# Moving the dense projections of three batched attentions to other heads, with V, k and output later in the narrow ones

## The reference

```python
x = x + jnp.tanh(g_xattn[1]) * _L1_xattn_ref(_layernorm(x, axis=-1), ctx_1024, ctx_1024, mask_BxS2_if1, 1, ...)
x = x + jnp.tanh(g_ffn[1]) * _L1_ffn_ref(_layernorm(x, axis=-1), ...)
```

```python
xn = _layernorm(x, ln_gamma, ln_beta)
q = (xn @ w_q).reshape(B, SQ, NUM_HEADS, DIM_HEAD)
kv = context @ w_kv
k, v = jnp.split(kv, 2, axis=-1)
...
scores = jnp.einsum('bqhd,bkhd->bhqk', q * SCALE, k)
attn = jax.nn.softmax(scores, axis=-1)
out = jnp.einsum('bhqk,bkhd->bqhd', attn, v).reshape(B, SQ, INNER)
out = out @ w_out + b_out
return out * jnp.tanh(gate[0])
```

## Time and profile before

| what | us |
|---|---|
| median of three runs | 3197.92 (3197.83 to 3222.6) |
| the profiled execution | 3205.33 |
| its span in the trace | 3203.5 |
| mean granted TensorE clock in it | 0.884 |
| PE busy, share of the span | 2656.1, 83% |
| DVE | 1589.6, 50% |
| ACT | 1262.7, 39% |
| POOL | 1249.5, 39% |

### The profile page before, as it was taken

One profiled execution on the slowest core, in us unless ns is written; L12 is line 12 of the kernel. 1 busy time (PEld: TensorE's weight loads), 2 busy tenths in 40 slices (PEclk: granted clock), 3 DMA queues, 4 the chain that ended last, 5 costly groups with the idle time before them and its releaser, 6 DMA issues. The chain is left out here.

```text
span 3203.5 us, 56229 instructions
## 1 busy us (share of the span) xinstructions
PE 2656.1 (83%) x18095; PEld 2431.6 (76%) x18096; DVE 1589.6 (50%) x3633; ACT 1262.7 (39%) x3098; POOL 1249.5 (39%) x1190
## 2 busy tenths in 40 slices
PE   4674479489989999869997289998899999789997
PEld 4574468388978888769896178887788888678887
DVE  3665545566625444455552234444677767333334
ACT  3232135144443333234444134443666666433332
POOL 0012461565322845032203555541354453284334
PEclk9786689698869999978885599999899999799999
DMA  3031244211001433110001233321000000042322
GB/s 114 1 132 47 81 159 134 61 46 40 9 30 54 145 95 111 40 44 28 28 8 40 86 101 108 118 80 40 17 22 19 13 13 7 27 142 90 111 69 89
DMA packets 128101, 207.99 MB, mean 65 GB/s; under 512 B 16576, under 2 KB 88412, under 8 KB 127728
## 3 DMA queue, kind: packets, MB, share of 16 engines
q1 hardware_dynamic: 63920, 119.94, 12.1%
q10 hardware_dynamic: 50064, 47.18, 4.6%
q0 software_dynamic: 13872, 37.66, 3.7%
HBM read 147.67 MB, written 57.02 MB: 64 GB/s over the span
## 5 line engine op out<-in xcount | busy, mean ns | idle before, releaser
L535 ACT ACTIVATE moe_act<-moe_gu 128x256 f32<-128x256 f32 (+1 forms) x431 | 189.3, 439 | 621.8 <-PE moe_gu L95 621.7
L93 PE MATMUL moe_gu<-moe_whi,moe_xThi 128*128 (+2 forms) x1018 | 409.6, 402 | 14.3 <-POOL moe_wlo L320 14.3
L93 PE MATMUL moe_yp<-moe_whi,moe_hThi 128*128 (+1 forms) x1238 | 394.1, 318 | 5.9 <-DVE moe_hTlo L821 5.6
L95 PE MATMUL moe_gu<-moe_whi,moe_xTlo 128*128 (+2 forms) x1018 | 390.3, 383 | 0.0
L94 PE MATMUL moe_gu<-moe_wlo,moe_xThi 128*128 (+2 forms) x1018 | 389.7, 383 | 0.0
L320 POOL TENSOR_TENSOR moe_wlo<-moe_raw,moe_whi 128x768 fp32r<-128x768 f32 (+1 forms) x174 | 350.5, 2015 | 37.8 <-issue 13.8
L94 PE MATMUL moe_yp<-moe_wlo,moe_hThi 128*128 (+1 forms) x1238 | 349.1, 282 | 0.0
L95 PE MATMUL moe_yp<-moe_whi,moe_hTlo 128*128 (+1 forms) x1238 | 349.0, 282 | 0.0
L821 DVE TENSOR_TENSOR moe_hTlo<-moe_tp,moe_hThi 128x256 fp32r<-128x256 f32 (+1 forms) x431 | 210.4, 488 | 236.5 <-ACT moe_hThi L541 234.8
L805 DVE TENSOR_TENSOR moe_h<-moe_act,moe_gu 128x256 f32<-128x256 f32 x321 | 135.0, 421 | 376.6 <-ACT moe_act L535 372.0
L318 POOL CAST moe_whi<-moe_raw 128x768 fp32r<-128x768 f32 (+1 forms) x174 | 156.5, 899 | 320.8 <-DMA moe_raw<-in_moe_w 320.3
(11 more groups left out here) (472 smaller groups left out, 6931.5 us busy)
## 6 DMA issues: line engine op xcount, KB each, us to landing
moe_raw<-in_moe_w SPq DMA_DIRECT2D x118, 384.0 KB, 3.2
moe_raw<-in_moe_w SPq DMA_DIRECT2D x56, 512.0 KB, 4.6
moe_xr<-rows_x ACTq DMA_DIRECT2D x69, 256.0 KB, 2.7
rows_y<-moe_y ACTq DMA_DIRECT2D x69, 256.0 KB, 2.2
rows_x<-att_zeros SPq DMA_DIRECT2D x16, 512.0 KB, 6.4
att_cT_hi<-ctxT_hi SPq DMA_DIRECT2D x24, 256.0 KB, 2.7
att_cT_lo<-ctxT_lo SPq DMA_DIRECT2D x24, 256.0 KB, 2.9
moe_xr<-rows_x ACTq DMA_DIRECT2D x41, 128.0 KB, 2.0
```

The source lines that it names most:

```text
L93: pe.matmul(out, lhs[0], rhs[0], start=first, stop=False, **kw)
L95: return pe.matmul(out, lhs[1], rhs[0], start=False, stop=last, **kw)
L535: act.activation(act_sb[i % 2][:, :], gu[i % 2][:, 0:HC], func).then_inc(act_done, 1)
```

## The change

In `wide_phase`:
- `kT` 3 and `qT` 3 of a batch are computed in its own heads 0 and 1, not in heads 13 and 14 of the one before. The other rounds move so that no head has more than one, but head 4, which has both `nT`; `V1` goes from heads 2 and 3 to 5 and 6. The context `cT` of the next batch is loaded after `V1`, as before.
- The output projection becomes two rounds at heads 2 and 3, one for each tile, in the banks `r_ps`. DVE adds each tile to x as its step of the round, ACT only reads a column of the bank into `seen`. `x_done` and its wait are gone; `o_hi` of the first pair waits until PE has done the second output round.
- The statistics for MoE are made at head 14 in place of 4; the expert rows are taken after heads 8, 10, 12 and 13 in place of 6, 12, 14 and 15; POOL makes the inverse roots at heads 14 and 15 of the batch before, and normalises at heads 0 and 1 in place of 1 and 2; its `add_bias` goes from head 9 to 10.

In `small_phase`:
- `v` goes from head 1 of its batch to head -3. Without rotation, `k` goes from -9 to -14 and `out` from 35 to 40 (from head 3 to head 8, two batches on). V has three buffers.
- The expert rows of batch 3 and later are taken 5 to 9 heads earlier: (-29, -26, -25, -25) for K = 2 and (-26, -25, -21, -16, -16) for K = 3. Batch 2 has its own list.
- POOL does `aux` for q and k ahead of `norm`.
- The statistics for MoE stand behind the round `out`.

The diff, cut to its core:

```diff
-    ROUNDS = [(4, "nT", 0), (5, "nT", 1), (7, "qT", 0), (8, "kT", 0), (8, "qT", 1), (9, "kT", 1), (10, "V0", 0), (10, "qT", 2),
-              (11, "kT", 2), (12, "V0", 1), (13, "qT", 3), (14, "kT", 3)]
-    OWN = [(2, "V1", 0), (3, "V1", 1)]
-    FIRST = [*(("kT", part) for part in range(4)), ("V0", 0), ("V0", 1), ("nT", 0), ("nT", 1), *(("qT", part) for part in range(4))]
+    ROUNDS = [(4, "nT", 0), (4, "nT", 1), (7, "qT", 0), (8, "kT", 0), (9, "qT", 1), (10, "kT", 1), (11, "V0", 0), (12, "V0", 1),
+              (13, "qT", 2), (14, "kT", 2)]
+    OWN = [(0, "kT", 3), (1, "qT", 3), (2, "out", 0), (3, "out", 1), (5, "V1", 0), (6, "V1", 1)]
+    FIRST = [*(("kT", part) for part in range(3)), ("V0", 0), ("V0", 1), ("nT", 0), ("nT", 1), *(("qT", part) for part in range(3))]
     PRO = len(ROUNDS)
...
-        TAKE = dict(zip((*((6, 12) if K == 2 else (6, 8, 12)), 14, 15), PIECES))
+        TAKE = dict(zip((*range(10 - 2 * (K - 1), 12, 2), 12, 13), PIECES))
...
-                    if h % 4 == 0:
+                    if h == 12:
+                        wait_own(pe, rd_done, i, lo, 0, "qT", 3, last)
+                    elif h % 4 == 0:
...
-                        if g == 1:
-                            wait(pe, x_done, i, lo, 1, s // H)
...
-                def project(i, lo, nxt):
-                    wait(pe, ol_done, i, lo, NGR, (nxt + 1) * NGR)
-                    out = o_ps[1][:, :].rearrange("p (t d) -> p t d", t=TB)
-                    for t in range(TB):
-                        for c in range(OC):
-                            mm = mm3(pe, out[:, t, :], [a[:, c, t * P:(t + 1) * P] for a in OT], [a[:, c, :] for a in wo], c == 0, c == OC - 1)
-                    mm.then_inc(out_ready, 1)
+                def project(bank, t):
+                    for c in range(OC):
+                        mm = mm3(pe, bank, [a[:, c, t * P:(t + 1) * P] for a in OT], [a[:, c, :] for a in wo], c == 0, c == OC - 1)
...
                     wait(pe, rd_done, i, lo, NRD, a + pos - 1)
-                    if kind == "nT":
+                    if kind == "out":
+                        if lo == 0:
+                            mm = pe.transpose(bank[:, 0:P], ident[:, :], ident[:, :])
+                        else:
+                            wait(pe, ol_done, i, lo, NGR, 0)
+                            mm = project(bank[:, 0:D], part)
...
-                        wait(act, out_ready, i, lo, 1, turn)
+                        wait(act, rd_ready, i, lo, NRD, PRO + turn * NRD + [r[1:] for r in BODY].index(("out", 1)) + 1)
...
+                    if kind == "out":
+                        act.activation(seen[:, part:part + 1], bank[:, 0:1], ACT.Copy).then_inc(rd_hi, 1)
...
-                def residual(b):
-                    v.wait_ge(out_ready, b + 1)
-                    v.wait_ge(biased, b + 1)
-                    out = o_ps[1][:, :].rearrange("p (t d) -> p t d", t=TB)
-                    v.scalar_tensor_tensor(x_of(b), out, tg[:, 0:1], x_of(b), ALU.mult, ALU.add).then_inc(x_done, 1)
+                def residual(b, t, src):
+                    if t == 0:
+                        v.wait_ge(biased, b + 1)
+                    xt = x[:, TB * b + t, :]
+                    return v.scalar_tensor_tensor(xt, src, tg[:, 0:1], xt, ALU.mult, ALU.add)
...
+                        if i == 0:
+                            v.drain().then_inc(rd_done, 1)
+                        else:
+                            residual(i - 1, part, bank[:, 0:D]).then_inc(rd_done, 1)
...
-                        if h == 3 and i > 0:
-                            residual(i - 1)
-                        if h == 4 and i > 0:
+                        if h == 14 and i > 0:
                             moments(i - 1)
...
-                        if i < B - 1:
-                            if h == 0:
-                                roots(i + 1, 0)
-                                roots(i + 1, 1)
-                            if h in (1, 2):
-                                norm(i + 1, 2 * h - 2)
-                                norm(i + 1, 2 * h - 1)
-                        if i < B - 2 and h in (3, 4):
-                            fetch(i + 2, h - 3)
-                        if h == 9:
+                        if i == 0 and h == 0:
+                            roots(1, 0)
+                            roots(1, 1)
+                        if i == 0 and h in (1, 2):
+                            norm(1, 2 * h - 2)
+                            norm(1, 2 * h - 1)
+                        if i < B - 2:
+                            if h in (3, 4):
+                                fetch(i + 2, h - 3)
+                            if h in (14, 15):
+                                roots(i + 2, h - 14)
+                        if 0 < i < B - 1 and h in (0, 1):
+                            norm(i + 1, 2 * h)
+                            norm(i + 1, 2 * h + 1)
...
-    plan = [(-11, "nT", 0), (-10, "q", 0), (-9, "k", 0), (1, "v", 0), (2, "qT", 0), (4, "kT", 0), (8, "qT", 1), (9, "kT", 1),
+    plan = [(-11, "nT", 0), (-10, "q", 0), (-9 if rotary else -14, "k", 0), (-3, "v", 0), (2, "qT", 0), (4, "kT", 0), (8, "qT", 1), (9, "kT", 1),
             (11, "qT", 2), (12, "kT", 2), (13, "qT", 3), (14, "kT", 3), (13, "mt", 0), (17, "mt", 1), (21, "mt", 2), (25, "mt", 3),
-            (26, "OT", 0), (34, "OT", 1), (35, "out", 0)]
-    own = [{("k", 0): -14, ("v", 0): -13, **{("kT", j): -12 for j in range(4)}, ("nT", 0): -10, ("q", 0): -9, ("v", 1): 1},
-           {("nT", 0): -7, ("q", 0): -6, ("k", 0): -5, ("qT", 0): 5, ("kT", 0): 6}] + [{}] * (B - 2)
+            (26, "OT", 0), (34, "OT", 1), (35 if rotary else 40, "out", 0)]
+    own = [{("k", 0): -14, ("v", 0): -13, **{("kT", j): -12 for j in range(4)}, ("nT", 0): -10, ("q", 0): -9},
+           {("nT", 0): -7, ("q", 0): -6, ("k", 0): -5, ("qT", 0): 5, ("kT", 0): 6}, {("k", 0): -9}] + [{}] * (B - 3)
...
-        for piece, off in zip([*range(K), "stats", "means"], (*((-21, -19) if K == 2 else (-22, -21, -19)), -16, -16)):
+        for q, piece in enumerate([*range(K), "stats", "means"]):
+            if b == 2:
+                off = (-20, -20, -20, -20)[q] if K == 2 else (-21, -20, -19, -16, -16)[q]
+            else:
+                off = (-29, -26, -25, -25)[q] if K == 2 else (-26, -25, -21, -16, -16)[q]
...
-        vp = [sb(f"vp{q}", [P, KC, H, dh + 1]) for q in range(2)]
+        vp = [sb(f"vp{q}", [P, KC, H, dh + 1]) for q in range(3)]
...
-                        if b >= 2:
-                            v.wait_ge(pv_done, 16 * (b - 1))
+                        if b >= 3:
+                            v.wait_ge(pv_done, 16 * (b - 2))
...
-                    if s >= 24 and s % 16 == 8:
-                        moments(s // 16 - 1)
-                moments(B - 1)
+                    for kind, b, part in rounds_at(s):
+                        if kind == "out":
+                            moments(b)
...
+                    aux(b, "q")
+                    aux(b, "k")
                     if b < B - 1:
                         norm(b + 1)
-                    aux(b, "q")
-                    aux(b, "k")
                     add_bias(b)
```

## The result

The changed kernel takes 3248.7 us (median of four, 3237.5 to 3267.6) beside 3199.3 of the kernel before: a ratio of 1.015, with a 95% interval of 1.010 to 1.020. The forecast was 3154, the range 3115 to 3192. The profiled execution took 3247.75 us.

The account below looks back on a forecast made before the run. PE was taken to bound the wide stage, with PE waits and low clock costing time in the narrow ones. Terms -25 (wide), -2 (narrow without clock) and -17 (clock) gave -44: 3197.9 becomes 3154 us, range 3115 to 3192.

Parts of the forecast that it names:

- Wide stage, -25: Wide attention: net 3.9 us a batch over six batches, 24, plus 1 from prologue and batch 0; -8 to -38.
- the 0.4 and 0.6 taken for late values and for DVE: Wide batch, added waits: transposes of head 5 late by 0.4 us, DVE's load in heads 7 to 15 costing 0.6.
- the 1.1 taken: Wide batch: mean clock of 0.98 costs 1.1 us, which goes with the waits.
- POOL's order, -2.0 us in four of five batches: Narrow attentions: aux ahead of norm removes the 2.0 us wait of qT 0 in four of five batches of either.
- Rows early: Narrow attentions: DVE waits 4.1 us (first), 3.1 (second) for rows; 2.5 and 2.2 reach PE; batch 0: 4.5 and 4.
- V at head 13: Narrow attentions: with V away from head 1, most of the 0.9 us wait for normalised values goes.
- The clock, -17: Narrow attentions: longest stretch without projections falls from ten heads to five, returning 12 of 34 and 5 of 21 us.
- The row that I called the one to remember: Second narrow attention, 1467 to 1491: PE busy 23.90 of 24.00 us, clock 0.61, over heads where no projection runs.
- Slower: the wait for rows: Rival, narrow attentions: DMAs land 3 us later, DVE's wait reaches PE whole, clock stays low; +41, 3239; chance 0.06.
- Rows in time: Rival, narrow attentions: rows land before DVE asks, nothing new waits; -26 more, 3128; chance 0.17.
- DVE becomes the bound: Rival, wide stage: batches only fall to 60 us and nothing else gains; -8, 3190; chance 0.12.
- Only the wide stage gains: Rival, narrow attentions: new waits drop the clock as the old did, narrow stages at 0; 3173; chance 0.20.

Follow-up runs that it names:

- rows_early: The base plus the expert rows of the narrow attentions taken where the changed kernel takes them: 3232.8 us, 1.0095 of before.
- the base: The kernel before with the new wide stage and POOL doing aux ahead of norm, other narrow code as before: 3153.5 us, 0.985 of before.
- rows_head10: The base with three pieces of rows of the first narrow attention after heads 8, 9, 10, not 10, 11, 13: 3307.3 us, 0.993 of before.
- k_out_late: The changed kernel with the expert rows of the narrow attentions taken after the same heads as before: 3316.9 us, 0.996 of before.
- aux_again: The base, run once more as the base of the third group: 3153.5 us, 0.985 of before.
- ot_head3: The base with transposes OT 1 at head 3, not 2, and output at head 4, not 3: 3256.0 us, 0.978 of before; again 3158.4 us, 0.983.
- aux_first: The kernel before with the new wide stage and POOL doing aux ahead of norm, first run: 3274.8 us, 0.973 of before.

## Why the prediction was wrong, point by point

**Wide stage, -25: right in the sum, by two errors that cancel.** 20.6 us in the stage and 4.1 ahead of it are 24.7. A batch fell by 3.7 us where 3.9 were worked out. The wait ahead of the output round is 0.7, as priced. But in place of the 0.4 and 0.6 taken for late values and for DVE stand 1.2 for nT 0, 0.9 for POOL's product and 0.4 for ACT, so the waits left are 3.2 and not 1.7. The clock of 0.98 did become 1.00, and that was worth more than the 1.1 taken: PE's busy time fell by 2.0 us a batch (338.90 to 327.06 in six).

**POOL's order, -2.0 us in four of five batches: right in place, too small.** The trace of before has this wait four times in attention 2 and three times in attention 1 (the text says four of five in either, the sum counts three for the first), 14 us in all, and all are gone. What this step had at nothing was the clock behind it: in attention 2 the five batches fell by 37.8 us (209.5 to 171.7), and only 8 of them are the wait. The last two batches gave 20 of that back. Over the kernel, wide stage and order together gave 51 us in the third group (3204.6 to 3153.5), so the order some 26.

**Rows early: the wait was over-sized, its price under-sized.** Landings were as worked out: the last gather of 741.17 released DVE at 744.00, 2.8 us after its issue, as the earlier trace rows has it. The heads ran later than I made them, so in the changed kernel DVE waited in six of ten batches, 2.3 to 3.0 us in attention 1 (forecast 4.1) and 1.4 to 1.9 in attention 2 (3.1). In `rows_early` PE got 2.2 and 1.7 (forecast 2.5 and 2.2; the terms of the second stage, 3.1 + 3.5 - 4.7, give 1.9), but mostly not from landings: where PE waited 2.2 us, DVE had waited for none, and a piece of rows took up to 2.4 us where 1.1 was priced. By lengths that is 20 us for the kernel. Measured alone it cost 79. The rest is low clock: 148 and 135 us of it in the two stages, against 60 and 71 in the base. Batch 0 of attention 1 shows the same: a forecast of 4.5 us, and 18 measured, with a low stretch of 34 us from head 10 on.

**V at head 13: two waits were missed.** I wrote that with V away from head 1 most of the 0.9 us for the normalised values would go. It grew to 1.5, because it was V's projection that kept PE busy until they were there. And I listed V as the round of head 13 without counting that qT 3 and mt 0 stand ahead of it with only two banks: 1.4 us. Together with their low clock, 44 us.

**The clock, -17: wrong, and this is the step that turned the sign.** I took the falls to be a matter of the longest stretch without a projection, cut that from ten heads (nine, counted by the list) to five on paper, and credited a part of 55 us. After the change there are 133 us more of low clock in the two stages. By the rate in the prediction (3.7 us for 3.9 of lost clock, that is 0.95, on half of 133) this is 63 us, beside a loss of 61.9. All idle pieces of PE over 0.2 us in the two stages grew only from 34.5 to 40.6 us.

What the runs show in place of that step has two parts. The first is waits. In attention 1 every fall in the eight traces of the faster groups (`before` and `after` among them) has waits of PE close ahead of it, 0.4 to 3.0 us together. The single edits show what such a wait costs among heads without projections: with 0.7 us at head 10, attention 2 of `rows_early` has a low stretch of 20 to 31 us in four batches, where the base has none in its five (`rows_head10` and `k_out_late` have the like, in slower groups). The change put such waits at heads 2, 5 to 10 and 13.

The second part is heads without projections alone, and here the prediction was right about before and wrong about after. The stretch of the earlier trace rows, last, began at 1472.5, and PE had waited for nothing in the 11 us ahead of it (the first row below). In the changed kernel four such heads behind V were enough: PE was busy throughout, the clock fell at 1528.3 for 20.5 us, and once more at 1702.4 (the second row):

```profile
1461.50:1472.50 11.00, 10.90 (x94) 10.51 (x95) 7.05 (x15) 3.97 (x9) 0.00 (x0) 1.00 0.01 2
1519.90:1528.30 8.40, 8.40 (x74) 8.38 (x75) 5.08 (x8) 4.45 (x8) 4.49 (x7) 1.00 0.21 65
```

So a shorter stretch doesn't keep the clock up. Nor does a long one always bring it down: the base has nine heads in a row without a dense projection in attention 2, and five batches at 1.00, then the fall at 1622.4. In the eight traces of attention 2, 17 of 41 falls have no idle piece of PE of 0.2 us or more close ahead of them. What decides between these cases is open.

Once the clock is down, PE fully busy with heads does not bring it back (17.10 of 17.10 and 64.80 of 64.80 us above); it came back just behind projections (in the kernel before with the exponents at heads 2, 4 or 7, and the projections at 1, 3, 6 and 7). An output projection alone, at head 3 of the last batch of `aux_again` (1656.1 to 1658.9), didn't bring it back. The change took V away from head 1, and its longest stretches last until head 7. The row that I called the one to remember showed how a low stretch lasts and that waits aren't needed for it; it didn't show that a shorter stretch would be safe, nor what a wait would add.

The Trainium skill (TensorE: Matmul & The Clock Gate, A second HAM failure mode: psum-queue depth-cycling) describes a kernel in which short idle times between groups of matmuls make the clock go back and forth. The traces of attention 1 agree, with 0.4 to 3.0 us of waits ahead of each fall; those of attention 2 only in part, as 17 of 41 falls stand behind no wait. In the prediction I weighed its sibling, gaps in which PE is idle, against one row and let the row decide; that was right for that row, but the new waits should have been priced by the rule as well.

**The rivals.** "Slower: the wait for rows" named a part of the mechanism, low clock behind a wait, and nearly the time (3239 against 3248.7), with a chance of 0.06. That the time is so near is luck: its condition, landings 3 us later and 5 us of wait beyond PE's cover, was not met. PE's waits were 0.7 to 2.2 us with landings as estimated, and V's move took a part (44 us when measured alone). "Rows in time" (0.17) held in seven of ten batches of `rows_early`, and gained nothing, since the pieces themselves stood in DVE's queue. "DVE becomes the bound" (0.12) did not happen. "Only the wide stage gains" had the right reason, that new waits drop the clock as the old ones did, but stopped at zero.

**What stays open.** Why in attention 2 the clock sometimes falls and sometimes holds over the same heads without any wait, and with it how much of the 133 us is due to waits and how much to the new places of the projections; whether k at head 2 and output at head 8 cost the 6.5 us a batch that the trace shows also in time; what the stops of ACT in the slower groups are. The single edits were measured against the base (79 and 44 us for rows and V) and don't simply add up to the changed kernel, which stands some 95 us above it by the ratios. That in those groups the changed kernel is at 0.994 and not 1.015 of before was measured once, with ten executions; that the stops are the reason is argued from the traces, not shown.

The best version, with `ot_head3` equal to it within the noise, is the new wide stage with POOL's new order and nothing else of the narrow edits: 0.985 (0.982 to 0.989), 0.983 (0.978 to 0.988) and 0.973 (0.966 to 0.980) of before in three groups, 3153.5 us where before took 3204.6.

## What to carry to other kernels

Price a wait of TensorE by what stands around it. Next to dense projections it cost its own length (0.8 us a batch for OT, where the clock held); among heads without projections, or right ahead of them, it can cost several times that (4 us more of waits and 71 us more of time in `rows_early`), since the clock fell and stayed down until the next group of projections. Don't take the rest for safe: the clock also fell over four such heads without any wait. Before work is spread out, list where the clock came back in the trace of before, and what stands at those places; a sum over five regular batches can mislead, as the last two gave back 20 of 38 us. And where loads or additions move ahead, count what they push back on their own engine's queue, even if no transfer is late: the first narrow attention of `rows_head10` took 329 us, that of `aux_first` 301, with every row in time.

## What was not expected of the hardware

The same kernel took 3336 and 3212 us in two groups on one and the same chip, and the traces of the slower groups have ACT standing for up to 30 us without a visible cause. And a long low stretch can have TensorE 95 to 100% busy: 42.3 of 44.4 us in attention 1 after the change, 17.1 of 17.1 in `k_out_late`, 64.8 of 64.8 in the base.
